# Second expert product of a mixture layer with the weights as the stationary side

## The chip, the cores and the metric

The program runs on one core of a Trainium2 chip. Its time is the device time of one execution, in microseconds (us). Of the kernel before, three timed runs gave 2428.65, 2429.38 and 2433.24 us; the median is 2429.38.

## What is computed

The program is a whole network on 3136 tokens (16 images of 14 x 14) of 256 channels: convolutions, a convolutional attention, and two layers of attention with a feed-forward part each. Only the last part, a mixture of experts, is touched:

```
logits = x @ router_w ; probs = softmax(logits)
gate = max(probs) ; idx = argmax(probs)
# each expert takes the first C = 3136/8 = 392 tokens that chose it, in "slots"
h = relu(expert_inputs @ w1[e] + b1[e])        # [392, 256] @ [256, 1024]
expert_outputs = h @ w2[e] + b2[e]             # [392, 1024] @ [1024, 256]
out[token] = gate[token] * expert_outputs[its slot]   # 0 for a token with no slot
x = x + out
```

There are 8 experts. All of it is float32. The experts' input is the layer-normalised x; their output is added to x itself.

## The kernel before

The function is `moe_ffn`. It is written out by hand as one program for each engine; semaphores alone set the order between engines, and each engine works through its own list strictly in order. In memory x lies with channels on partitions: 2 chunks of 128 channels (KC = 2), 3136 tokens along a row.

*Start.* The sync engine loads the router, b1 and b2 (L1992 to L1994, semaphore consts_in), then the weights of experts 0 and 1 (L1997, L1998). TensorE waits for all three small loads at the head of its list (consts_in at 48), takes the column means of the router (L2060) and turns b1 into columns (L2062). The vector engine subtracts the means from the router (L2182), and with that TensorE turns the tokens into rows and scores them (L2073, L2076), 128 tokens at a time. Slot numbers are worked out on the vector engine, and GpSimd scatters the normalised rows by slot into the DRAM tensor expert_in with 25 indirect DMAs (L2046). A row holds 256 channels, the token's number and its gate.

*Experts.* 392 slots are 4 groups (s) of 98 slots. Expert e uses buffers e % 2 of the weights w1 and w2, of the incoming rows ein, of the hidden layer h and of the result y. In order of TensorE's list:

- first product (L2104): for each of 8 blocks f of 128 hidden units, 2 matmuls into one of the banks 0 to 3, stationary a 128x128 piece of w1, moving the 392 slots. The activation engine adds b1 and clips (L2163) into h.
- second product (L2115): for each slot group s, 8 matmuls, stationary the 98 slots of h, moving the 256 channels of w2, into bank 6 or 7. The result has slots on partitions.
- between slot groups 2 and 3, `turn_in` (L2089): 8 transposes that bring the next expert's rows ein to channels on partitions (banks 4 and 5), copied out by the activation engine (L2152).

The vector engine makes the token numbers and gates of the expert (L2269 to L2275), multiplies b2 by the gates (b2g, L2278), and then, for each slot group, y = product x gate + b2g (L2284, semaphore y_ready). GpSimd scatters each slot group of y into out_rows by token number (L2053). When y_ready is full the sync engine loads ein and the weights of expert e + 2. Experts 0, 1 and 6, 7 are written out in TensorE's list, the others are in a loop.

*End.* When all scatters have landed (L2017), out_rows is loaded back in 8 pieces (L2019), turned by TensorE (L2128), added to x by the vector engine (L2292) and stored.

A float32 matmul shows in the trace as two records, each with a weight load of its own, a transpose as one.

Of the kernel before, what the change touches and what calls it, by code (L numbers as in the profile page):

```python
# [14 lines left out]
P = 128  # L15
# [14 lines left out]
def steps(eng, n, body):  # L30

    body(0)
    if n > 1:
        with eng.Fori(1, n) as i:
            body(i)
# [1877 lines left out]
def moe_ffn(nc, x, expert_in, out_rows, y_dram, mean_w, w, ident):  # L1913
# [15 lines left out]
    with Scope(nc, "moe") as S:  # L1929
# [14 lines left out]
        sent_f, sent = S.sb("sent_f", [P, NTILES]), S.sb("sent", [P, NTILES], U32)  # L1944
        w1 = [S.sb(f"w1_{p}", [P, KC, F]) for p in range(2)]
        w2 = [S.sb(f"w2_{p}", [P, KF, C]) for p in range(2)]
        b1_rows, b1, b2 = S.sb("b1_rows", [E * KF, P]), S.sb("b1", [P, E * KF]), S.sb("b2", [ST, E, C])
        ein = [S.sb(f"ein{p}", [ST, 4, CW]) for p in range(2)]
        token, gates = [S.sb(f"token{p}", [ST, 4], U32) for p in range(2)], [S.sb(f"gates{p}", [ST, 4]) for p in range(2)]
        vacant, token_f = S.sb("vacant", [ST, E, 4]), S.sb("token_f", [ST, 4])  # L1950
        b2g = S.sb("b2g", [ST, 4, C])
        ein_t = [S.sb(f"ein_t{p}", [P, KC, CAP]) for p in range(2)]
        h = [S.sb(f"h{p}", [P, KF, CAP]) for p in range(2)]
        y = [S.sb(f"y{p}", [ST, 4, C]) for p in range(2)]
# [15 lines left out]
        onehot_ready, counted, slots_ready = S.sem("onehot_ready"), S.sem("counted"), S.sem("slots_ready")  # L1970
        ein_turned, ein_ready, h_done, h_ready = S.sem("ein_turned"), S.sem("ein_ready"), S.sem("h_done"), S.sem("h_ready")
        token_step = S.sem("token_step")
        meta_ready, b2g_ready, y_done, y_ready = S.sem("meta_ready"), S.sem("b2g_ready"), S.sem("y_done"), S.sem("y_ready")
        back_turned, x_done = S.sem("back_turned"), S.sem("x_done")
        block = S.block()

# [13 lines left out]
        @block.sync  # L1990
        def _(sp):
            sp.dma_start(router[:, :, :], w["router_w"].rearrange("(k p) e -> p k e", p=P)).then_inc(consts_in, 16)  # L1992
            sp.dma_start(b1_rows[:, :], w["b1"].rearrange("e (f p) -> (e f) p", p=P)).then_inc(consts_in, 16)  # L1993
            sp.dma_start(b2[:, :, :], w["b2"].unsqueeze(0).broadcast_to([ST, E, C])).then_inc(consts_in, 16)  # L1994

            def weights(e, p):
                sp.dma_start(w1[p][:, :, :], w["w1"][bass.ds(e, 1)].rearrange("o (k p) f -> p (o k) f", p=P)).then_inc(w_in[p], 16)  # L1997
                sp.dma_start(w2[p][:, :, :], w["w2"][bass.ds(e, 1)].rearrange("o (k p) d -> p (o k) d", p=P)).then_inc(w_in[p], 16)  # L1998
            for p in range(2):
                weights(p, p)  # L2000
            sp.wait_ge(scattered, 16 * NTILES)
            for p in range(2):
                sp.dma_start(ein[p][:, :, :], slots_of(p)).then_inc(ein_in[p], 16)

            def body(i):
                for p in range(2):
                    e = 2 * i + p
                    sp.wait_ge(y_ready, 4 * (e + 1))
                    sp.wait_ge(ein_turned, e + 1)
                    sp.wait_ge(meta_ready, e + 1)  # L2010
                    sp.dma_start(ein[p][:, :, :], slots_of(e + 2)).then_inc(ein_in[p], 16)
                    weights(e + 2, p)
            body(0)
# [43 lines left out]
        def _(pe):  # L2057
# [1 line left out]
            for k in range(KC):  # L2059
                mm = nc.tensor.matmul(count_ps[:, 0:E], mean_w[:, :], router[:, k, :], start=(k == 0), stop=(k == KC - 1))  # L2060
            mm.then_inc(mean_done, 1)
            nc.tensor.transpose(bank[5][:, 0:E * KF], b1_rows[:, :], ident[0:E * KF, 0:E * KF]).then_inc(b1_turned, 1)  # L2062

            for g in range(NG):
                if g == 0:
# [27 lines left out]
            pe.wait_ge(ein_in[0], 16)  # L2093
            turn_in(0)

            def experts(i, last):
                for p in range(2):
                    e = 2 * i + p
                    pe.wait_ge(w_in[p], 32 * (i + 1))
                    pe.wait_ge(ein_ready, e + 1)  # L2100
                    for f in range(KF):
                        wait(pe, h_ready, KF * e + f - 3)
                        for k in range(KC):
                            mm = nc.tensor.matmul(a_ps[f % 4][:, 0:CAP], w1[p][:, k, f * P:(f + 1) * P], ein_t[p][:, k, :],  # L2104
                                                  start=(k == 0), stop=(k == KC - 1))
                        mm.then_inc(h_done, 1)
                    for s in range(4):
                        if s == 3 and not (last and p == 1):
                            pe.wait_ge(ein_in[1 - p], 16 * (i + 1 + p))
                            turn_in(1 - p)  # L2110
                        wait(pe, y_ready, 4 * e + s - 1)
                        for f in range(KF):
                            if s == 0:
                                pe.wait_ge(h_ready, KF * e + f + 1)
                            mm = nc.tensor.matmul(y_ps[s % 2][0:ST, 0:C], h[p][:, f, s * ST:(s + 1) * ST], w2[p][:, f, :],  # L2115
                                                  start=(f == 0), stop=(f == KF - 1))
                        mm.then_inc(y_done, 1)
            experts(0, False)
            with pe.Fori(1, E // 2 - 1) as i:
                experts(i, False)  # L2120
            experts(E // 2 - 1, True)

            for i in range(NPIECE):
                pe.wait_ge(back_in[i], 16)
# [7 lines left out]
        def _(act):  # L2132
            act.preload_act_table_set(LN_EXP)
            act.wait_ge(b1_turned, 1)
            nc.scalar.activation(b1[:, :], bank[5][:, 0:E * KF], ACT.Copy).then_inc(b1_ready, 1)
            for g in range(NG):
                js = group(g)
                a, b = js[0], js[-1] + 1
# [18 lines left out]
            def experts(i, last):  # L2157
                for p in range(2):
                    e = 2 * i + p
                    wait(act, y_done, 4 * (e - 1))  # L2160
                    for f in range(KF):
                        act.wait_ge(h_done, KF * e + f + 1)
                        nc.scalar.activation(h[p][:, f, :], a_ps[f % 4][:, 0:CAP], ACT.Relu, bias=b1[:, bass.ds(e * KF + f, 1)]).then_inc(h_ready, 1)  # L2163
# [9 lines left out]
        def _(dve):  # L2173
# [85 lines left out]
            chain.wait()  # L2259
            nc.vector.reciprocal(rows[:, :, C + 1], total[:, :]).then_inc(gate_ready, 1)  # L2260

            dve.wait_ge(consts_in, 48)

            def experts(i):
                for p in range(2):
# [8 lines left out]
                    nc.vector.tensor_copy(token[p][:, :], token_f[:, :])  # L2274
                    nc.vector.tensor_copy(gates[p][:, :], ein[p][:, :, C + 1]).then_inc(meta_ready, 1)  # L2275
                    dve.wait_ge(meta_ready, e + 1)
                    for s in range(4):
                        ins = nc.vector.tensor_scalar(b2g[:, s, :], b2[:, bass.ds(e, 1), :].rearrange("p o c -> p (o c)"),  # L2278
                                                      gates[p][:, s:s + 1], None, ALU.mult)
                    ins.then_inc(b2g_ready, 1)  # L2280
                    dve.wait_ge(b2g_ready, e + 1)
                    for s in range(4):
                        dve.wait_ge(y_done, 4 * e + s + 1)
                        nc.vector.scalar_tensor_tensor(y[p][:, s, :], y_ps[s % 2][0:ST, 0:C], gates[p][:, s:s + 1], b2g[:, s, :],  # L2284
                                                       ALU.mult, ALU.add).then_inc(y_ready, 1)
            steps(dve, E // 2, experts)

            for i in range(NPIECE):
                dve.wait_ge(back_turned, i + 1)
# [50 lines left out]
```

## Time and profile before

| | |
|---|---|
| median of three timed runs | 2429.38 us |
| profiled execution | 2433.36 us |
| its span, first to last instruction | 2431.3 us |
| mean granted clock of TensorE | 0.874 |
| TensorE busy over the span | 1915.6 us, 79% |
| vector engine busy | 1685.6 us, 69% |
| mixture stage, first DMA issue | 2105.93 us |
| first expert's first product | 2196.05 us |
| second product of the last expert ends | 2397.97 us |

The mixture stage is the last 325 us of the span, and the eight experts are 202 us of it. Times inside the trace count from the start of the span. Nothing outside `moe_ffn` is edited, so the shares over the whole span say little here; the views that are cut to the last 325 us do.

### The profile page before, as it was taken

How to read it: one execution, taken by the hardware profiler on the slowest of the kernel's cores; microseconds unless marked ns; L12 is line 12 of the kernel's file. 1: busy time of each engine (PE TensorE's matmuls, PEld its weight loads, DVE VectorE, ACT ScalarE, POOL GpSimd, SP SyncE). 2: the span in 40 equal slices, each digit the busy share in tenths (PEclk: the TensorE clock that was granted, in tenths of full speed). 3: DMA queues.
4: the chain of work that ended last, by engine and by line, in shares of the span. 5: the costliest groups of instructions: out<-in, count | busy, mean ns of one | idle time of the engine just before them, and what ended most of it. 6: DMA issues, size and time to landing. Idle time of an engine off the chain costs nothing. (4 is left out here: it accounts for less than half of the span.)

```text
span 2431.3 us, 48421 instructions
## 1 busy us (share of the span) xinstructions
PE 1915.6 (79%) x17730; PEld 1571.1 (65%) x17730; DVE 1685.6 (69%) x7003; ACT 669.6 (28%) x1492; POOL 463.1 (19%) x667
## 2 busy tenths in 40 slices
PE   7595899984569788797787977878869699728996
PEld 3364688872468677676676766767758577526674
DVE  3333666634999999989989998999995577321112
ACT  2342355543222131121311213112120255321210
POOL 2002344330020202202112021120220300041110
PEclk8786999996789899898998989989879899858997
DMA  2222444413500000000000000000000333312434
GB/s 59 80 84 58 113 109 101 103 23 99 113 6 5 2 6 1 6 6 1 6 2 6 5 2 6 1 6 2 1 2 1 74 84 83 96 52 69 139 99 116
DMA packets 90505, 111.10 MB, mean 46 GB/s; under 512 B 27166, under 2 KB 79070, under 8 KB 89534
## 3 DMA queue, kind: packets, MB, share of 16 engines
q1 hardware_dynamic: 84752, 99.88, 15.6%
q0 software_dynamic: 3344, 6.53, 0.8%
q8 instruction: 144, 2.36, 0.4%
q10 hardware_dynamic: 2176, 1.61, 0.2%
q14 instruction: 89, 0.73, 0.1%
HBM read 70.63 MB, written 33.83 MB: 43 GB/s over the span
## 5 line engine op out<-in xcount | busy, mean ns | idle before, releaser
L1618 PE MATMUL peer_out_ps<-peer_g,peer_up 128*128 128x256 f32 (+1 forms) x1664 | 378.1, 392 | 84.6 <-issue 76.7
L1618 PEld LDWEIGHTS peer_out_ps<-peer_g,peer_up 128*128 128x128 f32 x1664 | 326.0, 203 | 133.0 <-issue 84.7
L1583 PE MATMUL peer_x_ps<-peer_xc,peer_dt 128*128 128x256 f32 (+1 forms) x1664 | 355.2, 374 | 26.8 <-DMA peer_up<-in_L_ffn_expert_up_dram 19.0
L1583 PEld LDWEIGHTS peer_x_ps<-peer_xc,peer_dt 128*128 128x128 f32 x1664 | 308.2, 192 | 68.6 <-issue 28.6
L1547 POOL TENSOR_TENSOR peer_g<-peer_g,peer_qt 128x512 f32<-128x512 f32 x96 | 153.9, 1644 | 802.8 <-ACT peer_qt L1709 802.8
L1687 ACT ACTIVATE peer_g<-peer_x_ps 128x512 f32<-128x512 f32 (+1 forms) x208 | 119.1, 572 | 645.7 <-PE peer_x_ps L1583 645.6
L1284 DVE TENSOR_REDUCE l_attn_mx<-l_attn_s_ps 98x4 f32<-98x392 f32 (+1 forms) x320 | 175.0, 560 | 140.3 <-PE l_attn_s_ps L1054 101.0
L1607 PE MATMUL peer_x_ps<-peer_oh_h,peer_oh_a 128*128 128x32 bf16 x3136 | 171.5, 181 | 112.3 <-DVE peer_oh_l L1875 96.4
L1607 PEld LDWEIGHTS peer_x_ps<-peer_oh_h,peer_oh_a 128*128 128x128 bf16 x3136 | 165.1, 99 | 129.5 <-DVE peer_oh_l L1875 64.7
L1868 DVE TENSOR_TENSOR peer_oh_a<-peer_a_t,peer_iota_f 128x8192 bf16<-128x8192 bf16 x49 | 216.7, 4423 | 1.3
L1205 ACT ACTIVATE l_attn_pt<-l_attn_st_ps 98x392 f32<-98x392 f32 x320 | 148.1, 491 | 146.4 <-PE l_attn_st_ps L1067 145.6
L1732 DVE FIND_INDEX8 peer_i<-peer_v,peer_sc 128x8 uint32<-128x64 f32 (+1 forms) x800 | 175.4, 236 | 0.0
L1608 PE MATMUL peer_x_ps<-peer_oh_l,peer_oh_a 128*128 128x32 bf16 x3136 | 170.6, 181 | 0.0
L1608 PEld LDWEIGHTS peer_x_ps<-peer_oh_l,peer_oh_a 128*128 128x128 bf16 x3136 | 165.2, 99 | 0.9
L1050 PE MATMUL l_attn_s_ps<-l_attn_stk,l_attn_stq 96*98 96x196 bf16 (+1 forms) x768 | 112.4, 243 | 31.5 <-DMA l_attn_stk<-l_attn_pieces_k_dram 19.0
L2284 DVE SCALAR_TENSOR_TENSOR moe_y<-moe_b_ps,moe_gates,moe_b2g 98x256 f32<-98x256 f32 x32 | 15.5, 484 | 174.3 <-PE moe_b_ps L2115 174.3
L979 POOL TENSOR_SCALAR_AFFINE_SELECT l_attn_pt<-l_attn_pt 98x196 f32<-98x196 f32 (+1 forms) x192 | 98.6, 519 | 136.6 <-ACT l_attn_pt L1205 135.3
L1067 PE MATMUL l_attn_st_ps<-l_attn_stq,l_attn_stk 98*98 98x196 bf16 (+1 forms) x768 | 111.5, 243 | 9.2 <-ACT l_attn_pt L1205 4.5
L1727 DVE MAX8 peer_v<-peer_sc 128x8 f32<-128x64 f32 (+1 forms) x800 | 106.0, 215 | 11.1 <-issue 9.8
L2115 PE MATMUL moe_b_ps<-moe_w,moe_h 128*98 128x256 f32 x512 | 113.0, 379 | 0.0
L2115 PEld LDWEIGHTS moe_b_ps<-moe_w,moe_h 128*98 128x98 f32 x512 | 83.9, 165 | 26.9 <-issue 1.3
L1050 PEld LDWEIGHTS l_attn_s_ps<-l_attn_stk,l_attn_stq 96*98 96x98 bf16 x768 | 71.7, 128 | 43.7 <-DVE l_attn_mx L1284 22.0
(318 smaller groups left out, 3520.8 us busy)
## 6 DMA issues: line engine op xcount, KB each, us to landing
moe_w<-in_L_ffn_w_dram SPq DMA_DIRECT2D x16, 1024.0 KB, 8.7
l_attn_pieces_q_dram<-l_attn_pieces_q SPq DMA_DIRECT2D x16, 294.0 KB, 4.6
l_attn_pieces_k_dram<-l_attn_pieces_k SPq DMA_DIRECT2D x16, 294.0 KB, 3.2
l_attn_stq<-l_attn_pieces_q_dram SPq DMA_DIRECT2D x16, 294.0 KB
l_attn_stk<-l_attn_pieces_k_dram SPq DMA_DIRECT2D x16, 294.0 KB
peer_g<-n_L_ffn_expert_down_dram SPq DMA_DIRECT2D x8, 512.0 KB
peer_up<-in_L_ffn_expert_up_dram SPq DMA_DIRECT2D x2, 2048.0 KB
moe_expert_in<-l_blank SPq DMA_DIRECT2D x16, 197.5 KB
```

The costliest lines, as they stand in the source:

```text
L1050: mm = nc.tensor.matmul(out[:, j, :], stq[n % NB][0:KS, spot(h), t * TH:(t + 1) * TH], stk[n % NB][0:KS, spot(h), 0:nb * TH], start=(j == ...
L1205: nc.scalar.activation(pt[g % NPT][:, f * FW:(f + 1) * FW], st_ps[i % 2][0:TH, 0:FW], ACT.Exp).then_inc(exp_done, 1)
L1284: nc.vector.tensor_reduce(mx[n % 2][:, hs[0]:hs[0] + len(hs), t], s_ps[i % 2][0:TH, 0:FW].rearrange("p (h j) -> p h j", j=nb * TH), AX_X, ...
L1547: nc.gpsimd.tensor_tensor(g[:, :, ts], g[:, :, ts], m_copy[q % 2].rearrange("p (t j) -> p j t", j=J), ALU.mult).then_inc(g_done_late, 1)
L1583: mm = nc.tensor.matmul(x_ps[b][:, jj * CT:jj * CT + cols], dt[:, k, 2 * jp + jj, :], xc[p][:, k, 0:cols], start=(k == 0), stop=(k == KC - 1))
L1607: nc.tensor.matmul(x_ps[q][:, i * J:(i + 1) * J], oh_a[hb % 2][:, t, :], oh_h[hb % 2][:, t, :], start=True, stop=False)
L1608: mm = nc.tensor.matmul(x_ps[q][:, i * J:(i + 1) * J], oh_a[hb % 2][:, t, :], oh_l[hb % 2][:, t, :], start=False, stop=True)
L1618: mm = nc.tensor.matmul(out_ps[:, m * CT:m * CT + cols], up[:, j, m * P:(m + 1) * P], g[:, j, 0:cols], start=(j == 0), stop=(j == J - 1))
L1687: nc.scalar.activation(g[:, 2 * jp:2 * jp + 2, 0:cols], x_ps[jp % 4][:, 0:2 * CT].rearrange("p (j t) -> p j t", j=2)[:, :, 0:cols], ACT.Ge ...
L1732: last = nc.vector.max_index(indices[:, q, r], values[:, q, r], source)
L1868: nc.vector.tensor_tensor(view(oh_a[q]), spread(a_t, P), number(P), ALU.is_equal)
L2115: mm = nc.tensor.matmul(y_ps[s % 2][0:ST, 0:C], h[p][:, f, s * ST:(s + 1) * ST], w2[p][:, f, :], start=(f == 0), stop=(f == KF - 1))
```

## The change

The second product swaps its sides: the stationary piece is 128x128 of w2 (128 hidden units, 128 channels), and all 392 slots of h move. There are two such products per expert, one for each chunk k of 128 channels, into banks 6 and 7. The result has channels on partitions, so b2 becomes a column of 128 and is added by the vector engine as it moves the bank into a new buffer yt; b2 is loaded as 16 rows of 128 and turned like b1. The scatter needs slots on partitions, so yt is turned back: `turn_out`, 8 transposes into banks 4 and 5, and the vector engine multiplies by the gate on the way into y (`slots_out`). For expert e, turn_out stands in expert e + 1, after block f = 1 of its first product, and slots_out after the token work of e + 1; for the last expert both stand at the end. turn_in moves between the two channel chunks and waits for y_ready of the expert before, since it uses the same banks. The sync engine asks for the next rows and weights at y_done instead of y_ready.

```diff
-            sp.dma_start(b2[:, :, :], w["b2"].unsqueeze(0).broadcast_to([ST, E, C])).then_inc(consts_in, 16)
+            sp.dma_start(b2_rows[:, :], w["b2"].rearrange("e (k p) -> (e k) p", p=P)).then_inc(consts_in, 16)
...
-                    sp.wait_ge(y_ready, 4 * (e + 1))
+                    sp.wait_ge(y_done, KC * (e + 1))
...
+            def turn_out():
+                for half in range(2):
+                    for s in range(2 * half, 2 * half + 2):
+                        for k in range(KC):
+                            o = (s % 2) * C + k * P
+                            mm = nc.tensor.transpose(t_ps[half][0:ST, o:o + P], yt[:, k, s * ST:(s + 1) * ST], ident[:, :])
+                    mm.then_inc(y_turned, 1)
...
                         mm.then_inc(h_done, 1)
-                    for s in range(4):
-                        if s == 3 and not (last and p == 1):
+                        if f == 1 and not first:
+                            pe.wait_ge(yt_ready, KC * e)
+                            turn_out()
+                    for k in range(KC):
+                        if k == 1 and not (last and p == 1):
                             pe.wait_ge(ein_in[1 - p], 16 * (i + 1 + p))
+                            wait(pe, y_ready, 4 * e)
                             turn_in(1 - p)
-                        wait(pe, y_ready, 4 * e + s - 1)
+                        wait(pe, yt_ready, KC * e)
                         for f in range(KF):
-                            if s == 0:
+                            if k == 0:
                                 pe.wait_ge(h_ready, KF * e + f + 1)
-                            mm = nc.tensor.matmul(y_ps[s % 2][0:ST, 0:C], h[p][:, f, s * ST:(s + 1) * ST], w2[p][:, f, :],
+                            mm = nc.tensor.matmul(y_ps[k][:, 0:CAP], w2[p][:, f, k * P:(k + 1) * P], h[p][:, f, :],
                                                   start=(f == 0), stop=(f == KF - 1))
                         mm.then_inc(y_done, 1)
...
+            pe.wait_ge(yt_ready, KC * E)
+            pe.wait_ge(y_ready, 4 * (E - 1))
+            turn_out()
...
+            def slots_out(e, p):
+                for s in range(4):
+                    dve.wait_ge(y_turned, 2 * e + s // 2 + 1)
+                    nc.vector.tensor_scalar(y[p][:, s, :], t_ps[s // 2][0:ST, (s % 2) * C:(s % 2 + 1) * C], gates[p][:, s:s + 1], None,
+                                            ALU.mult).then_inc(y_ready, 1)
...
-                    for s in range(4):
-                        ins = nc.vector.tensor_scalar(b2g[:, s, :], b2[:, bass.ds(e, 1), :].rearrange("p o c -> p (o c)"),
-                                                      gates[p][:, s:s + 1], None, ALU.mult)
...
-                        nc.vector.scalar_tensor_tensor(y[p][:, s, :], y_ps[s % 2][0:ST, 0:C], gates[p][:, s:s + 1], b2g[:, s, :],
-                                                       ALU.mult, ALU.add).then_inc(y_ready, 1)
+                    if not (isinstance(e, int) and e == 0):
+                        slots_out(e - 1, 1 - p)
+                    for k in range(KC):
+                        dve.wait_ge(y_done, KC * e + k + 1)
+                        wait(dve, y_turned, 2 * e)
+                        nc.vector.tensor_scalar(yt[:, k, :], y_ps[k][:, 0:CAP], b2[:, bass.ds(e * KC + k, 1)], None, ALU.add).then_inc(yt_ready, 1)
             steps(dve, E // 2, experts)
+            slots_out(E - 1, 1)
```

TensorE's list before, from the end of the first product of expert 0 to the third block of expert 1's. A name b4 is bank 4; the form at the end is that of the output.

```order
L2104 MATMUL moe_b3_ps<-moe_ein_t0,moe_w1_0 128x392 x2
L2115 MATMUL moe_b6_ps<-moe_w2_0,moe_h0 98x256 x8
L2115 MATMUL moe_b7_ps<-moe_w2_0,moe_h0 98x256 x8
L2115 MATMUL moe_b6_ps<-moe_w2_0,moe_h0 98x256 x8
L2089 MATMUL moe_b4_ps<-net_ident,moe_ein1 128x98 x4
L2089 MATMUL moe_b5_ps<-net_ident,moe_ein1 128x98 x4
L2115 MATMUL moe_b7_ps<-moe_w2_0,moe_h0 98x256 x8
L2104 MATMUL moe_b0_ps<-moe_ein_t1,moe_w1_1 128x392 x2
L2104 MATMUL moe_b1_ps<-moe_ein_t1,moe_w1_1 128x392 x2
L2104 MATMUL moe_b2_ps<-moe_ein_t1,moe_w1_1 128x392 x2
```

The same place now:

```order
L2116 MATMUL moe_b3_ps<-moe_ein_t0,moe_w1_0 128x392 x2
L2131 MATMUL moe_b6_ps<-moe_h0,moe_w2_0 128x392 x8
L2092 MATMUL moe_b4_ps<-net_ident,moe_ein1 128x98 x4
L2092 MATMUL moe_b5_ps<-net_ident,moe_ein1 128x98 x4
L2131 MATMUL moe_b7_ps<-moe_h0,moe_w2_0 128x392 x8
L2116 MATMUL moe_b0_ps<-moe_ein_t1,moe_w1_1 128x392 x2
L2116 MATMUL moe_b1_ps<-moe_ein_t1,moe_w1_1 128x392 x2
L2104 MATMUL moe_b4_ps<-net_ident,moe_yt 98x128 x4
L2104 MATMUL moe_b5_ps<-net_ident,moe_yt 98x128 x4
L2116 MATMUL moe_b2_ps<-moe_ein_t1,moe_w1_1 128x392 x2
```

32 matmuls of 256 columns became 16 of 392, and the transposes out of yt (L2104 of the new text) stand behind two blocks of the next first product.

The vector engine's list before, for expert 1:

```order
L2269 SCALAR_TENSOR_TENSOR moe_token_f<-moe_ein1,moe_vacant 98x4
L2272 TENSOR_TENSOR moe_token_f<-moe_token_f,moe_ein1 98x4
L2274 CAST moe_token1<-moe_token_f 98x4
L2275 COPY moe_gates1<-moe_ein1 98x4
L2278 TENSOR_SCALAR moe_b2g<-moe_b2,moe_gates1 98x256 x4
L2284 SCALAR_TENSOR_TENSOR moe_y1<-moe_b6_ps,moe_gates1,moe_b2g 98x256
L2284 SCALAR_TENSOR_TENSOR moe_y1<-moe_b7_ps,moe_gates1,moe_b2g 98x256
L2284 SCALAR_TENSOR_TENSOR moe_y1<-moe_b6_ps,moe_gates1,moe_b2g 98x256
L2284 SCALAR_TENSOR_TENSOR moe_y1<-moe_b7_ps,moe_gates1,moe_b2g 98x256
```

And now:

```order
L2295 SCALAR_TENSOR_TENSOR moe_token_f<-moe_ein1,moe_vacant 98x4
L2298 TENSOR_TENSOR moe_token_f<-moe_token_f,moe_ein1 98x4
L2300 CAST moe_token1<-moe_token_f 98x4
L2301 COPY moe_gates1<-moe_ein1 98x4
L2287 TENSOR_SCALAR moe_y0<-moe_b4_ps,moe_gates0 98x256 x2
L2287 TENSOR_SCALAR moe_y0<-moe_b5_ps,moe_gates0 98x256 x2
L2308 TENSOR_SCALAR moe_yt<-moe_b6_ps,moe_b2 128x392
L2308 TENSOR_SCALAR moe_yt<-moe_b7_ps,moe_b2 128x392
```

The slots of expert 0 (y0) are written in expert 1's turn, before the two channel halves of expert 1 itself.

## Rows read from the trace of the kernel before

**Rows 1.** Chain of waits: start us, length us, what, from the first expert on
```profile
2196.05 12.93 PE moe_b_ps L2104 x32
2208.98 10.36 PE moe_b_ps L2115 x48
2219.34 0.68 PE moe_b_ps L2089 x8
2220.02 3.46 PE moe_b_ps L2115 x16
2223.47 10.53 PE moe_b_ps L2104 x32
...
2384.16 10.37 PE moe_b_ps L2115 x48
```

**Rows 2.** Stretches: length; busy us PE, PEld, DVE, ACT, POOL; PE clock; DMA; GB/s
```profile
2106.00:2112.00 6.00, 0.02 (x1) 0.02 (x1) 0.06 (x1) 1.22 (x1) 1.37 (x7) 0.50 0.62 192
2112.00:2145.00 33.00, 30.80 (x155) 30.49 (x155) 12.88 (x61) 12.32 (x33) 0.00 (x0) 0.50 0.34 119
2196.00:2198.00 2.00, 1.95 (x3) 1.18 (x4) 0.00 (x0) 0.00 (x0) 0.00 (x0) 0.50 0.00 0
2222.00:2247.00 25.00, 25.00 (x105) 17.29 (x104) 3.68 (x12) 5.58 (x10) 3.79 (x4) 1.00 0.37 116
```

**Rows 3.** Instructions on the PSUM banks: ns min/median/max, first and last start
```profile
L2115 PEld LDWEIGHTS moe_b_ps<-moe_w,moe_h x512: 163/165/167, 2208.5 to 2397.4; 128*98 128x98 f32 x171
L2104 PEld LDWEIGHTS moe_b_ps<-moe_ein_t,moe_w x256: 190/190/338, 2196.0 to 2383.3; 128*128 128x128 f32 x128
L2089 PE MATMUL moe_b_ps<-net_ident,moe_ein x64: 245/248/396, 2193.4 to 2369.9; 98*128 98x98 f32 x64
```

**Rows 4.** Timeline at the end of the last first product: start, length, instruction
```profile
2384.19 0.59 ACT L2163 ACTIVATE moe_h<-moe_b_ps,moe_b 128x392 f32<-128x392 f32 x1 [0.73 <-PE moe_b_ps L2104]
```

**Rows 5.** Timeline at the start of the stage
```profile
2106.97 0.57 SPq L1994 DMA_DIRECT2D moe_b<-in_L_ffn_b_dram  x1
2111.98 1.02 PE L2060 MATMUL moe_b_ps<-moe_router,net_mean_w 128*128 128x8 f32 x4 [7.89 <-DMA moe_b<-in_L_ffn_b_dram]
2113.47 0.69 PE L2073 MATMUL moe_b_ps<-net_ident,net_x 128*128 128x128 f32 x2 [0.17 <-DVE moe_centred L2182]
```

**Rows 6.** DMA issues (KB each, us to landing), and the group of GpSimd's scatters
```profile
l_wn<-in_L_conv_Wf_dram SPq DMA_DIRECT2D x1, 64.0 KB, 2.0
moe_w<-in_L_ffn_w_dram SPq DMA_DIRECT2D x16, 1024.0 KB, 8.7
L2046 POOL DMA_INDIRECT moe_expert_in<-moe_rows,moe_sent x25 | 24.4, 977 | 56.0 <-DVE moe_rows L2260 48.7 <-issue 7.3
```

**Rows 7.** Timeline of the last expert's second product and after, and the chain's wait
```profile
2383.99 13.98 PE L2115 MATMUL moe_b_ps<-moe_w,moe_h 128*98 128x256 f32 x64
2387.65 0.48 DVE L2284 SCALAR_TENSOR_TENSOR moe_y<-moe_b_ps,moe_gates,moe_b2g 98x256 f32<-98x256 f32 x1 [11.65 <-PE moe_b_ps L2115]
2388.96 0.95 POOL L2053 DMA_INDIRECT moe_out_rows<-moe_y,moe_token  x1 [13.57 <-DVE moe_y L2284]
2398.01 0.48 DVE L2284 SCALAR_TENSOR_TENSOR moe_y<-moe_b_ps,moe_gates,moe_b2g 98x256 f32<-98x256 f32 x1 [2.97 <-PE moe_b_ps L2115]
2398.79 0.94 POOL L2053 DMA_INDIRECT moe_out_rows<-moe_y,moe_token  x1 [2.50 <-DVE moe_y L2284]
2401.57 0.02 SPq L2017
```

**Rows 8.** Groups of the vector engine: busy, mean ns of one | idle before
```profile
L1250 DVE TENSOR_TENSOR l_attn_xn<-l_attn_xn,l_attn_rstd 128x392 f32<-128x392 f32 x32 | 17.9, 558 | 9.9 <-ACT l_attn_rstd L1165 9.9
L2284 DVE SCALAR_TENSOR_TENSOR moe_y<-moe_b_ps,moe_gates,moe_b2g 98x256 f32<-98x256 f32 x32 | 15.5, 484 | 174.3 <-PE moe_b_ps L2115 174.3
L506 DVE TENSOR_SCALAR l_lin<-l_c_ps,l_scale,l_shift 64x392 f32<-64x392 f32 x8 | 5.5, 693 | 0.0
L507 DVE TENSOR_SCALAR l_ypad<-l_lin 64x392 f32<-64x392 f32 x8 | 2.9, 361 | 0.3
```

More of the change, by code:

```diff
@@ L1946, in moe_ffn @@
         w2 = [S.sb(f"w2_{p}", [P, KF, C]) for p in range(2)]
-        b1_rows, b1, b2 = S.sb("b1_rows", [E * KF, P]), S.sb("b1", [P, E * KF]), S.sb("b2", [ST, E, C])
+        b1_rows, b1 = S.sb("b1_rows", [E * KF, P]), S.sb("b1", [P, E * KF])
+        b2_rows, b2 = S.sb("b2_rows", [E * KC, P]), S.sb("b2", [P, E * KC])
         ein = [S.sb(f"ein{p}", [ST, 4, CW]) for p in range(2)]
@@ L1950, in moe_ffn @@
         vacant, token_f = S.sb("vacant", [ST, E, 4]), S.sb("token_f", [ST, 4])
-        b2g = S.sb("b2g", [ST, 4, C])
+        yt = S.sb("yt", [P, KC, CAP])
         ein_t = [S.sb(f"ein_t{p}", [P, KC, CAP]) for p in range(2)]
@@ L1972, in moe_ffn @@
         token_step = S.sem("token_step")
-        meta_ready, b2g_ready, y_done, y_ready = S.sem("meta_ready"), S.sem("b2g_ready"), S.sem("y_done"), S.sem("y_ready")
+        meta_ready, y_done, y_ready = S.sem("meta_ready"), S.sem("y_done"), S.sem("y_ready")
+        yt_ready, y_turned = S.sem("yt_ready"), S.sem("y_turned")
         back_turned, x_done = S.sem("back_turned"), S.sem("x_done")
@@ L2061, in _ @@
             mm.then_inc(mean_done, 1)
-            nc.tensor.transpose(bank[5][:, 0:E * KF], b1_rows[:, :], ident[0:E * KF, 0:E * KF]).then_inc(b1_turned, 1)
+            nc.tensor.transpose(bank[5][:, 0:E * KF], b1_rows[:, :], ident[0:E * KF, 0:E * KF])
+            nc.tensor.transpose(bank[5][:, E * KF:E * KF + E * KC], b2_rows[:, :], ident[0:E * KC, 0:E * KC]).then_inc(b1_turned, 1)
             for g in range(NG):
@@ L2098, in experts @@
                     e = 2 * i + p
+                    first = isinstance(e, int) and e == 0
                     pe.wait_ge(w_in[p], 32 * (i + 1))
@@ L2134, in _ @@
             act.wait_ge(b1_turned, 1)
-            nc.scalar.activation(b1[:, :], bank[5][:, 0:E * KF], ACT.Copy).then_inc(b1_ready, 1)
+            nc.scalar.activation(b1[:, :], bank[5][:, 0:E * KF], ACT.Copy)
+            nc.scalar.activation(b2[:, :], bank[5][:, E * KF:E * KF + E * KC], ACT.Copy).then_inc(b1_ready, 1)
             for g in range(NG):
@@ L2159, in experts @@
                     e = 2 * i + p
-                    wait(act, y_done, 4 * (e - 1))
+                    wait(act, y_done, KC * (e - 1))
                     for f in range(KF):
@@ L2260, in _ @@
             nc.vector.reciprocal(rows[:, :, C + 1], total[:, :]).then_inc(gate_ready, 1)
-            dve.wait_ge(consts_in, 48)
+            dve.wait_ge(b1_ready, 1)
+            def slots_out(e, p):
[3 more added lines that the diff above has]
+                                            ALU.mult).then_inc(y_ready, 1)
             def experts(i):
@@ L2276, in experts @@
                     dve.wait_ge(meta_ready, e + 1)
-                    for s in range(4):
-                        ins = nc.vector.tensor_scalar(b2g[:, s, :], b2[:, bass.ds(e, 1), :].rearrange("p o c -> p (o c)"),
-                                                      gates[p][:, s:s + 1], None, ALU.mult)
[L2280 to L2283, printed above, removed]
-                        nc.vector.scalar_tensor_tensor(y[p][:, s, :], y_ps[s % 2][0:ST, 0:C], gates[p][:, s:s + 1], b2g[:, s, :],
-                                                       ALU.mult, ALU.add).then_inc(y_ready, 1)
+                    if not (isinstance(e, int) and e == 0):
[4 more added lines that the diff above has]
+                        nc.vector.tensor_scalar(yt[:, k, :], y_ps[k][:, 0:CAP], b2[:, bass.ds(e * KC + k, 1)], None, ALU.add).then_inc(yt_ready, 1)
             steps(dve, E // 2, experts)
+            slots_out(E - 1, 1)
             for i in range(NPIECE):
```

## The prediction

> **What bounds the kernel now.** I read four views, from the coarse to the fine. The chain of waits, in order of time, comes first: from 2196 to 2398 us, through all eight experts, every link of it is TensorE, and the links join end to start. One expert is 10.53 us for the first product (32 records, two to each float32 matmul), 10.36 + 3.46 us for the second (64 records) and 0.68 us for the eight transposes of the next expert's rows, 25.03 us in all [rows 1]. So whatever TensorE does not have to do there comes off the time, and nothing else on another engine does, unless TensorE is made to wait for it. The stretches with the granted clock say the same: in 25 us TensorE is busy 25.00 us at clock 1.00, the vector engine 3.68, the activation engine 5.58, GpSimd 3.79 [rows 2]. The view of the instructions on the PSUM banks gives the price of a record and of its weight load [rows 3]. The timelines of the two ends of the stage show what stands before the first expert and after the last [rows 5, 7].
>
> **Second product.** Before: 64 records of 256 columns in 13.82 us, 216 ns each, 0.84 ns a column. After: 16 matmuls, 32 records, of 392 columns, in the same form as the first product (128x128 stationary, 392 columns moving), and 32 of those take 10.53 us, 329 ns each and again 0.84 ns a column [rows 1]. The gain is one of columns, 16,384 against 12,544: with 98 slots as the stationary side 30 of the 128 columns of the array stood empty, with 128 channels none does. The weight load grows from 165 to 190 ns but stays under a record of 329 ns, as it does in the first product [rows 3]. 8 x (13.82 - 10.53) = 26.3 us less. Bounds: the form is in the trace, so I allow 0.1 us an expert at the joints, 25.5 to 26.5. The waits for h_ready move from every 0.43 us to every 0.66 us, and the activation that they wait for takes 0.59 us in both; the last one is asked for 14 records after the first product ends, 4.6 us, and it is there after 0.62 [rows 4]. No cost.
>
> **Turning back, seven times inside the next expert.** Eight transposes of 128 columns. The eight of turn_in, 98 columns each, add 0.68 us between two products, 85 ns each though one lasts 248 [rows 1, 3]; by columns 128/98 x 85 = 111 ns, 0.89 us for eight. From below it is 0.68 (pace set by the issue, not the columns), from above eight full durations in a row, 8 x 0.25 = 2.0. I take 0.9, since turn_in is the same operation in the same surroundings: 7 x 0.9 = 6.3 us more, ends 4.8 and 14.
>
> The rows show such transposes overlapping, so they are priced by pace. The Trainium skill (TensorE: Matmul & The Clock Gate, Part 4: PE-mode transpose) gives about 275 ns for one inside a kernel; laid end to end that would be 2.2 us an expert, an estimate from that page, and 9 us more than in my sum. This trace disagrees for turn_in, with 85 ns of pace against 248 of duration.
>
> **Does TensorE wait for it?** turn_out stands behind four records of the next first product, 4 x 0.33 = 1.32 us after the second product ended. By then the vector engine must have moved the second channel half out of PSUM. It starts 0.04 us after the last matmul today [rows 7] and its work is new in this form: one operand from PSUM, 128x392, float32. Nearest rows: 361 ns for such a shape out of SBUF, 558 for two operands of 128x392, 693 for a two-step operation out of PSUM [rows 8]. I take 0.56; with 0.69 it is still 0.6 us early. It stands ahead of the token work in the vector engine's program, so nothing is queued before it. The next wait, turn_in for y_ready, comes after the whole first product and half of the second, some 15 us after turn_out, while slots_out is four operations of at most 0.5 us [rows 8]. The scatters of an expert now run in the first third of the next one, at one per 1.27 us [rows 6]; their buffers are asked for again one expert later. The weights are asked for at y_done, half a microsecond earlier than at y_ready, and land after 8.7 us [rows 6], while the period shrinks only from 25.0 to 22.6. So the covers hold, all of them by at least 0.6 us. The removed b2g work, four short operations an expert under the first product, was hidden and gives nothing back.
>
> **Start of the stage.** TensorE waits until 2111.98 for b2, 784 KB broadcast to 98 partitions, issued at 2106.97 [rows 5]. Now b2 is 16 rows of 512 bytes, 8 KB. Transfers of 64 KB land 2.0 us after their issue in this kernel [rows 6], so consts_in should be full at about 2109.3, 2.7 us earlier. From below nothing is gained (the router load, 8 KB in small pieces, could be the late one), from above 3.0 (the load of b1 issued half a microsecond before must land too). One more transpose of 16 rows stands before router_ready, where TensorE had 0.17 us to spare [rows 5], so 0.1 us back. Everything behind it, scores, slots, 25 scatters at 1.27 us, is a chain of waits that moves as a whole. The clock there is already at 0.50 before the stage starts and stays [rows 2], so nothing changes in it. I take 2.6 us less.
>
> **Tail, once.** Before: the last matmul ends at 2397.97, the vector engine takes 0.48, GpSimd starts its last scatter at 2398.79 and the wait for the scatters ends at 2401.57, 3.60 us after the matmul [rows 7]. The other three scatters were done during the second product, one slot group every 3.45 us. Now all four come after it: 0.04 + 0.56 for the second channel half into SBUF; 0.03 + 0.75 until the first four transposes are through (weight load 0.17, duration 0.25, three at 0.11); 0.50 for the first slots into y; 0.84 until GpSimd starts, as it does at the first scatter of an expert today (2388.13 to 2388.96 [rows 7]); then three more scatters at 1.27 = 3.81 [rows 6]; and 2.77 from the start of the last to its landing. Together 9.30 us, so 5.7 more. Ends: 5.0 with 0.30 in place of 0.84 and the smallest vector times, 6.3 with the largest. The eighth turn_out is in here. From the load of out_rows on nothing changes.
>
> **Sum** against the profiled execution (2433.36 us, span 2431.3): -26.3 + 6.3 - 2.6 + 5.7 = -16.9 us, 2416.5. That execution stands 4.0 us above the median of the three timed runs, 2429.38, which spread over 4.6 us while the stage changed here has the same instructions in each; I subtract from the median: 2412.5 us.
>
> **Rivals.**
> A. The transposes of turn_out don't overlap: 2.0 us an expert instead of 0.9, 7.8 us more, 2420.3. For it: their stationary side comes from a tile just written and their bank pair was last read by the activation engine. Against it: turn_in is under the same conditions. 0.06.
> B. The load of b2 was not what held the start, and the router's small pieces were: 2.6 us are not gained, 2415. For it: a name in the trace covers only the transfer that ended last, and nothing shows when the router landed. Against it: 784 KB from the end of their issue at 2107.54 to 2111.98 are 181 GB/s, close to the 192 GB/s that the stretch from 2106 to 2112 shows [rows 2, 5]. 0.12.
> C. TensorE waits at turn_out because the channel half comes late. It takes more than 1.32 us from the last matmul to yt_ready; each 0.5 us over it costs 3.5, so 2416 to 2420. Only an operation of twice the 0.69 us gets there. 0.04.
> D, the other side: the clock falls. After turn_out (and turn_in) TensorE's clock drops from 2.4 to 1.2 GHz. A fall has a price in this trace: the first expert's first product, begun at clock 0.50, takes 12.93 us instead of 10.53, 2.40 more [rows 1, 2]. One fall at each of the seven turn_out gives back 16.8, which is no change (2429.3); with eight transposes more at turn_in falling too, that is fifteen falls, 36 us, and 2448. It is slower from the eighth fall on. Against it: the stretch of 25 us with turn_in in its middle stays at 1.00 [rows 2], and turn_out adds only 0.9 us of the same kind, with matmuls on both sides. 0.04, half of it past the eighth fall.
>
> Rival D is what a rule would make of it: the Trainium skill (TensorE: Matmul & The Clock Gate, Part 4: PE-mode transpose) says that the full clock does not engage for transposes, since they do not count as busy in the same way. By that rule the trace agrees where only transposes and 8-column products run (0.50 throughout), and does not where they stand among long matmuls.
>
> **How the numbers follow.** My forecast, 2412.5, has 0.72; A 0.06, B 0.12, C 0.04, D 0.04, and 0.02 is left for something in the tail or elsewhere that I don't see. The forecast's own range, from the ends of its terms that can fall together (start 1 to 3 us, turn_out 4.8 to 8, tail 5.0 to 6.3), and 1 us for the spread of a median of three, is 2409 to 2416. To hold 8 in 10 it reaches to B and to the near part of C: 2408.5 to 2417.5. What counts as a change is 0.2%, 4.9 us, about what a measurement of this kernel can tell from none. Faster than 2424.5: the forecast, B, C, A, together 0.94; within: the half of D up to the eighth fall and half of the rest, 0.03; slower: the other halves, 0.03.
>
> **What would show it.** In the changed kernel's chain: the second product as 8 x 32 records in 10.5 us, an expert in 22.6 us, turn_out with 0.9 us between two parts of the first product and no idle time of TensorE before it. At the start: L2062 (the first matmul of the stage) some 2.7 us earlier after the barrier. At the end: four scatters spaced 1.27 us after the last matmul and 9.3 us until the loads of out_rows. Wrong if an expert takes over 23.5 us, if the clock in it is under 1.00, if the matmul at the start comes at the same distance from the barrier, or if the tail is outside 8.5 to 10 us.

## The result and the profile after

The changed kernel takes 2413.3 us (median of 6 runs), the one before 2429.02 in the same series: ratio 0.993, 95% interval 0.9911 to 0.9949. Two later series gave 0.9902 (0.9863 to 0.9941) and 0.9919 (0.9889 to 0.9949). It is faster by 0.7 to 1.0% by the three ratios and by 16 to 20 us by the medians; 2412.5 had been forecast. One execution, of the kernel both_ends below, took 4707.02 us where all others lie between 2401 and 2439; it is left out of every median and ratio here, and its cause is open.

Single runs of either kernel differ by up to 19 us, so the terms are read inside the stage. Its four pieces, in us, each the difference of two starts in a timeline:

| profile | first issue to first matmul | to first product of expert 0 | to load of out_rows | to end of span | stage |
|---|---|---|---|---|---|
| before | 6.05 | 84.07 | 205.57 | 29.7 | 325.4 |
| after | 2.84 | 83.83 | 190.95 | 29.4 | 307.0 |

The chain of waits after, from expert 0 on (start us, length us, what); L2131 is the second product, L2092 turn_in, L2104 turn_out:

```profile
2186.20 12.78 PE moe_b_ps L2116 x32
2198.98 5.27 PE moe_b_ps L2131 x16
2204.25 0.68 PE moe_b_ps L2092 x8
2204.92 5.29 PE moe_b_ps L2131 x16
2210.22 2.63 PE moe_b_ps L2116 x8
2212.85 0.88 PE moe_b_ps L2104 x8
2213.72 7.90 PE moe_b_ps L2116 x24
...
2357.50 10.55 PE moe_b_ps L2131 x32
```

Against [rows 1]: the second product is 5.27 + 5.29 = 10.56 us where it was 13.82, turn_out is 0.88 between two parts of the first product, every link is TensorE and none waits. An expert is 22.64 us instead of 25.03. The clock stays up. Over one period of an expert the vector engine is busy 3.38 us in 10 operations, where it was 3.68 us in 12 (the last line of [rows 2], whose 25.00 us are one period of the kernel before; columns as there):

```profile
2210.22:2232.86 22.64, 22.64 (x81) 13.62 (x81) 3.38 (x10) 5.58 (x10) 3.80 (x4) 1.00 0.38 128
```

How much cover turn_out has is in the timeline. The second product ends at 2210.22 by the chain, and the vector engine's move of the second channel half ends at 2210.88:

```profile
2210.25 0.63 DVE L2308 TENSOR_SCALAR moe_yt<-moe_b_ps,moe_b 128x392 f32<-128x392 f32 x1 [5.26 <-PE moe_b_ps L2131]
2212.69 1.04 PE L2104 MATMUL moe_b_ps<-net_ident,moe_yt 128*98 128x128 f32 x8
```

Two blocks of the first product are eight records, 2.63 us, and the move is through 0.66 us after the second product: 1.97 us are to spare in the chain.

The start, in the timeline, for [rows 5]:

```profile
2099.53 0.40 SPq L1994 DMA_DIRECT2D moe_router<-in_L_ffn_router_w_dram  x1
2100.57 0.58 SPq L1996 DMA_DIRECT2D moe_b_rows<-in_L_ffn_b_dram  x1
2102.37 1.02 PE L2062 MATMUL moe_b_ps<-moe_router,net_mean_w 128*128 128x8 f32 x4 [4.68 <-DMA moe_b_rows<-in_L_ffn_b_dram]
2103.86 0.69 PE L2076 MATMUL moe_b_ps<-net_ident,net_x 128*128 128x128 f32 x2
```

TensorE still waits for a bias load (the name stands for b1_rows and for b2_rows), but b2 is now 8 KB (L1996), and the first matmul comes 1.80 us after its issue. The additional transpose costs nothing: 1.49 us from L2062 to L2076, as before. The tail, for [rows 7]:

```profile
2357.33 10.70 PE L2131 MATMUL moe_b_ps<-moe_h,moe_w 128*128 128x392 f32 x32
2368.18 0.62 DVE L2308 TENSOR_SCALAR moe_yt<-moe_b_ps,moe_b 128x392 f32<-128x392 f32 x1 [4.64 <-PE moe_b_ps L2131]
2368.86 1.08 PE L2104 MATMUL moe_b_ps<-net_ident,moe_yt 128*98 128x128 f32 x8 [0.83 <-DVE moe_yt L2308]
2369.54 1.66 DVE L2287 TENSOR_SCALAR moe_y<-moe_b_ps,moe_gates 98x256 f32<-98x256 f32 x4 [0.74 <-PE moe_b_ps L2104]
2370.85 0.95 POOL L2055 DMA_INDIRECT moe_out_rows<-moe_y,moe_token  x1 [15.56 <-DVE moe_y L2287]
2372.10 0.94 POOL L2055 DMA_INDIRECT moe_out_rows<-moe_y,moe_token  x1 [0.31 <-issue]
2373.35 0.95 POOL L2055 DMA_INDIRECT moe_out_rows<-moe_y,moe_token  x1 [0.30 <-issue]
2374.60 0.95 POOL L2055 DMA_INDIRECT moe_out_rows<-moe_y,moe_token  x1 [0.30 <-issue]
2377.15 6.50 SPq L2021 DMA_DIRECT2D moe_back<-moe_out_rows  x8
```

The last matmul ends at 2368.03. The vector engine is through with all four slot groups at 2371.20, but GpSimd's fourth scatter starts only at 2374.60: the tail is a queue on GpSimd. 9.12 us to the load of out_rows, where it was 3.65.

### The profile page after: what moved, and what is told of

It is laid out like the page before. It is cut to its first block and busy times, and to the rows that moved or that the text cites. A ratio compares the mean times of both kernels' runs of the same rounds, so it can differ in the third digit from the quotient of the medians.

```text
span 2406.5 us, 48028 instructions
## 1 busy us (share of the span) xinstructions
PE 1891.0 (79%) x17539; PEld 1540.1 (64%) x17539; DVE 1684.0 (70%) x6987; ACT 670.1 (28%) x1493; POOL 462.3 (19%) x667
## 5 line engine op out<-in xcount | busy, mean ns | idle before, releaser
L1732 DVE FIND_INDEX8 peer_i<-peer_v,peer_sc 128x8 uint32<-128x64 f32 (+1 forms) x800 | 166.0, 219 | 0.0
L2308 DVE TENSOR_SCALAR moe_yt<-moe_b_ps,moe_b 128x392 f32<-128x392 f32 x16 | 10.0, 625 | 146.1 <-PE moe_b_ps L2131 146.1
L1088 PE MATMUL l_attn_o_ps<-l_attn_pt,l_attn_va 98*32 98x196 f32 (+1 forms) x1536 | 91.9, 309 | 9.5 <-DVE l_attn_o L1291 8.9
L1067 PEld LDWEIGHTS l_attn_st_ps<-l_attn_stq,l_attn_stk 98*98 98x98 bf16 x768 | 70.7, 125 | 39.6 <-ACT l_attn_pt L1205 13.4
```

Source lines behind the costliest of these rows:

```text
L1067: mm = nc.tensor.matmul(out[:, j, :], stk[n % NB][:, spot(h), u * TH:(u + 1) * TH], stq[n % NB][:, spot(h), t0 * TH:HW], start=(j == 0), s ...
L1732: last = nc.vector.max_index(indices[:, q, r], values[:, q, r], source)
```

## The experiments

All were compared by the four pieces of the stage:

| profile | first matmul | to first product | to load of out_rows | to end | stage |
|---|---|---|---|---|---|
| after_again | 2.95 | 84.13 | 190.94 | 30.8 | 308.8 |
| after_long | 3.00 | 84.14 | 191.05 | 28.9 | 307.1 |
| start_alone | 2.45 | 83.84 | 205.71 | 29.5 | 321.5 |
| turn_first | 2.99 | 84.53 | 197.90 | 28.2 | 313.6 |
| turn_four | 2.90 | 84.12 | 209.47 | 28.9 | 325.4 |
| halves_all | 2.78 | 84.35 | 191.48 | 28.2 | 306.8 |
| narrow | 2.90 | 84.57 | 190.93 | 27.5 | 305.9 |
| tail_halves | 2.91 | 84.96 | 187.88 | 29.3 | 305.1 |
| both_ends | 2.00 | 84.40 | 188.55 | 27.9 | 302.8 |
| both_again | 1.70 | 84.58 | 188.46 | 28.2 | 302.9 |

The third piece is the steady one: the unedited changed kernel shows it three times within 0.11 us. What moves in it is the first product of expert 0, which begins at clock 0.50 (in the changed kernel 0.50 up to 2190, 0.88 from there to 2191 and 1.00 behind it) and takes 12.52 to 13.24 us over all these profiles with the same instructions. Without it the piece is 178.17, 178.18 and 178.18 us in the three profiles of the changed kernel; where a difference is given "less expert 0's first product" below, it is taken so. The last piece, the stores of the output, varies by 3 us over all these profiles.

**The changed kernel again** (after_again and after_long, no edit).

> The changed kernel once more, unedited. Two theories on why its timed runs spread over 11 us (2408.4 to 2419.5) where those of the kernel before spread over 5. Theory 1: the spread comes from the part of the program that was not edited (the first layers, up to the first load of the attention part at 225.9 us in the one profile of the changed kernel and 233.9 us in that of before), and the mixture stage, from its first DMA issue to the end of the span, is 307.0 us again, to within 0.5 us, whatever the whole time is. Theory 2: the new overlap in the stage is unsteady (scatters and weight loads at the same time), and the stage differs by several us between the profiles.

Four runs, 2403.9 to 2419.3, median 2409.98. The stage began at 2104.28, 4.8 us later than in the first profile, and 13 runs of the kernel before spread over 19 us in this series: the spread belongs to the unedited part and to both kernels (theory 1), though the stage itself moved by 1.8 us, more than the 0.5 expected, 1.4 of it in the stores. The piece with the new overlap stood still (190.94 against 190.95), so theory 2 falls.

> The changed kernel unedited, timed in five rounds on one chip beside the next kernel and the kernel before, because single runs of all of them differ by up to 19 us in the part that was not edited. Theory: the difference to the kernel before is the difference of the stages in the profiles, 325.4 less 307.0 to 308.8, so 16.6 to 18.4 us, ratio 0.9925 to 0.993; stage again 307 to 309. Rival: something outside the stage gained or lost too; then the ratio of many runs lies away from 0.993 by more than its interval.

Six runs, median 2410.0, ratio 0.9919 (0.9889 to 0.9949). The stages differ by 16.6 to 18.4 us in three profiles, a ratio of 0.9932 to 0.9924, inside the interval. No sign of a gain or loss outside the stage; the interval would hide one of up to some 7 us.

**The start alone** (start_alone, edit of the kernel before):

```diff
-            sp.dma_start(b2[:, :, :], ...).then_inc(consts_in, 16)      # before the weights
+            sp.dma_start(b2[:, :, :], ...).then_inc(b2_in, 16)          # behind the weights
-            pe.wait_ge(consts_in, 48)
+            pe.wait_ge(consts_in, 32)
```

> The kernel before, with one part of the change alone: the broadcast load of b2 no longer stands in front of TensorE (it is issued behind the weights, with a semaphore of its own, and the vector engine waits for it before the experts). The experts are as before. My theory: the start term was a wait for these 784 KB alone, so the stage gets 3.2 us shorter (from the first issue to the first matmul 2.8 us instead of 6.05), stage 322.2 instead of 325.4 us, whole time 2426. Rival: the router's small pieces or the crowd of weight loads behind them hold the start; then the first matmul comes at 4 to 6 us after the first issue and the stage is 324 to 325 us.

The first matmul comes 2.45 us after the first issue, the experts are as before (205.71), the stage is 3.9 us shorter (3.2 expected); ten timed runs against 13 give 0.9981 (0.9962 to 0.9999), median 2426.83. 3.6 of the 6.05 us were the wait for the broadcast b2; the router's pieces and the weight loads issued behind it held nothing up beyond that. The rival falls. With b2_rows still in front the changed kernel starts 0.4 to 0.55 us later than this one profile (2.84 to 3.00 in three), so the 8 KB of b2 do not look free either.

**turn_out without cover** (turn_first, edit of the changed kernel): the call moved from behind block f = 1 to before block f = 0.

> The changed kernel with the eight transposes back (turn_out) ahead of the next expert's first product instead of behind its second block: the cover of 1.32 us is gone. My theory: TensorE then waits, seven times, for the move of the second channel half out of PSUM, 0.04 + 0.62 us after the last matmul, plus the start of a weight load and the drain, 0.8 to 0.9 us each time as at the end of the stage (0.83 us of idle there): 5.6 to 6.3 us more, an expert 23.5 us instead of 22.65, stage 312.6 to 313.3 instead of 307.0. Rival: the move is no matter at this place, since the sequencer hides it: stage within 1 us of 307.0.

```profile
2219.93 0.62 DVE L2308 TENSOR_SCALAR moe_yt<-moe_b_ps,moe_b 128x392 f32<-128x392 f32 x1 [5.26 <-PE moe_b_ps L2131]
2220.70 1.05 PE L2104 MATMUL moe_b_ps<-net_ident,moe_yt 128*98 128x128 f32 x8 [0.81 <-DVE moe_yt L2308]
```

6.95 us more, and 7.2 in the piece less expert 0's first product (185.38 against 178.17), 1.03 for each of seven: TensorE is idle for 0.7 to 0.9 us, and the eight transposes take 1.05 to 1.08 us in the chain where they took 0.88. Above the 5.6 to 6.3 expected, since I had counted the idle time alone. The cover that was taken away is 2.63 us, two blocks of four records each, and not 1.32 as I had written; one block, 1.31 us, would by these rows still cover the 0.66 us that the move needs, but no run shows that. The cover is worth 7 of the 16 to 20 us.

**turn_out four times over** (turn_four, edit: the eight transposes listed four times before each signal, in the seven calls inside the experts).

> The changed kernel with each of the seven turn_out inside the experts done four times over (32 transposes in a row, the same result written four times; the last turn_out, at the end, once). Theory of pace: a transpose of 128 columns costs 0.11 us of TensorE wherever it stands, so 7 x 24 x 0.109 = 18.3 us more, stage 325.3 us, clock 1.00 throughout the experts. Rival, the clock: 3.5 us of nothing but transposes let TensorE's clock fall to 1.2 GHz; then at least 2.4 us more for each expert, 35 us or more in all, and a granted clock under 1.00 in the stretches of the experts. Rival, durations: if they did not overlap it would be 0.27 each, 46 us.

The chain of one expert and a stretch:

```profile
2236.92 2.63 PE moe_b_ps L2116 x8
2239.56 3.49 PE moe_b_ps L2104 x32
2243.05 7.90 PE moe_b_ps L2116 x24
```
```profile
2235.00:2260.00 25.00, 25.00 (x104) 16.06 (x103) 3.47 (x10) 5.58 (x10) 3.78 (x4) 1.00 0.35 117
```

32 transposes in 3.49 us, 109 ns each, clock 1.00: 18.5 us more in the third piece, 18.3 less expert 0's first product; 18.3 expected. Rivals A (no overlap) and D (the clock falls) both fall, and D by four times the dose.

**Twice the records and weight loads** (halves_all, edit: each matmul of the second product as two of 196 columns).

> The changed kernel with every second-product matmul cut in two, 196 columns each with a weight load of its own: the same columns, twice the records and weight loads (64 records an expert, as many as in the kernel before). Theory of columns: 64 x 196 x 0.84 ns + 3 ns each = 10.7 us instead of 10.55, so 1 to 2 us more over eight experts, 192 to 193 us from the first product to the load of out_rows instead of 190.9. Rival, weight loads: a record can't be shorter than the 190 ns of its weight load; then 12.2 us an expert, 13 us more, 204. That rival would also make the number of weight loads, halved by the change, a cause of the gain.

```profile
2227.10 5.31 PE moe_b_ps L2133 x32
```
```profile
L2133 PEld LDWEIGHTS moe_b_ps<-moe_h,moe_w x512: 190/190/192, 2203.9 to 2373.6; 128*128 128x128 f32 x171
```

64 records of 196 columns take 5.31 + 5.33 = 10.64 us, 166 ns each, though each weight load lasts 190: loads overlap each other. The rival's 12.2 us falls. It is 0.5 us more in all (0.6 less expert 0's first product), under the 1 to 2 expected: 2.5 ns for each of the 256 additional records. The halved number of records and weight loads is therefore 0.6 us of the gain at most.

**A narrower stationary side** (narrow, edit: 14 of 16 matmuls of a second product load 98 of the 128 channels; 30 channels are left out of the sum there).

> The changed kernel with 14 of the 16 matmuls of each second product loading only 98 of the 128 channels as their stationary piece (30 channels are left out of the sum there). Theory: the time goes by the columns that move, 392, and not by how full the array is, so the second product takes 10.5 us again and the stage is unchanged within 0.3 us from first product to the load of out_rows (190.9): 98 stationary columns in the kernel before cost as much per moving column as 128, and the emptiness was the loss. Rival: a narrower stationary side is cheaper in itself, 98/128 of the time, 8.1 us an expert; then the stage is 16 to 19 us shorter.

```profile
L2132 PEld LDWEIGHTS moe_b_ps<-moe_h,moe_w x256: 165/165/192, 2202.6 to 2371.3; 128*98 128x98 f32 x112, 128*128 128x128 f32 x16
```
```profile
2225.71 5.27 PE moe_b_ps L2132 x16
```

The weight load is back at 165 ns, the product takes 5.27 us for 16 records as with 128 channels, the third piece is 190.93, and the rival's 8.1 us falls. In this product the time goes by the columns that move. Together with the last run this settles the main term.

**Both ends.** tail_halves changes the last expert (shortened):

```diff
+    for part in range(2):                       # 196 slots each; banks 6, 7 and then 0, 1
+        for k in range(KC):
+            if part == 1 and k == 1:
+                pe.wait_ge(yt_ready, KC * e + 2)
+                pe.wait_ge(y_ready, 4 * e)
+                turn_out((0,))                  # slot groups 0 and 1
+            for f in range(KF): matmul(..., w2[...], h[p][:, f, cols])
...
+            pe.wait_ge(yt_ready, KC * E + 2)
+            turn_out((1,))
```

> The changed kernel, the last expert's second product in two halves of 196 slots (second half in banks 0 and 1), the first half turned back after the first product of the second half, so that two of the four last scatters are done under it. Theory: the tail is a queue on GpSimd, four scatters at 1.25 us. Two of them go under the product; TensorE ends 0.6 us later (four transposes moved in, records of 196 columns), and from its last matmul to the load of out_rows there are 5.9 us instead of 9.1. From the first product of expert 0 to that load 188.3 us instead of 190.9. Rival: GpSimd is late anyway through the vector engine, which serves both halves in order; then it is 190 to 191.

```profile
2371.39 0.95 POOL L2055 DMA_INDIRECT moe_out_rows<-moe_y,moe_token  x1 [11.95 <-DVE moe_y L2302]
2372.64 0.94 POOL L2055 DMA_INDIRECT moe_out_rows<-moe_y,moe_token  x1 [0.31 <-issue]
2374.67 0.95 POOL L2055 DMA_INDIRECT moe_out_rows<-moe_y,moe_token  x1 [1.08 <-DVE moe_y L2302]
2375.93 0.95 POOL L2055 DMA_INDIRECT moe_out_rows<-moe_y,moe_token  x1 [0.30 <-issue]
2378.47 6.87 SPq L2021 DMA_DIRECT2D moe_back<-moe_out_rows  x8
```

187.88 us, 3.1 less; 2.8 of it is the edit's (175.35 against 178.17 less expert 0's first product), 2.6 were expected. TensorE's last matmul ends at 2372.70, and 5.77 us later out_rows is loaded (5.9 expected, 9.12 in the changed kernel). both_ends adds to it a start in which TensorE waits for the router alone and turns the biases after the first group of tokens (shortened):

```diff
-            sp.dma_start(b1_rows[:, :], ...).then_inc(consts_in, 16)
+            sp.dma_start(b1_rows[:, :], ...).then_inc(bias_in, 16)      # b2_rows too
-            pe.wait_ge(consts_in, 48)
+            pe.wait_ge(consts_in, 16)
```

> The changed kernel with both ends worked on. At the start the biases b1 and b2 no longer stand before the first matmul: TensorE waits for the router alone, and turns the biases after the first four groups of tokens. At the end the last expert's second product is done in two halves of 196 slots, the second half in banks 0 and 1, and the first half is turned back, gated and scattered while the second is computed. Expected as the sum of the two single kernels: 0.9 us at the start and 2.6 at the end, stage 303.5 to 305.3 instead of 307.0 to 308.8, so 3.5 us under the changed kernel and some 20 to 22 us under the one before (2408 against 2429.5). Rival: the two halves cost TensorE more than the scatters give back, and the whole is within 1 us of the changed kernel.

> The kernel with both ends worked on, unedited, in the same rounds. Theory: its stage is 302.8 us again to within 1.5 us, 4 to 5 us under the changed kernel, and so is the median, 2407 to 2409 where the changed kernel has 2411 to 2413. The difference is as large as what the timed runs can tell, so the stage decides. Rival: same median as the changed kernel, the gain of the two ends being lost in the stores of the output, whose landing varied by 3 us between profiles.

The stage is 302.8 and 302.9 us, 4 to 6 under the changed kernel and under the 303.5 to 305.3 expected. The first matmul comes after 2.00 and 1.70 us. The experts are as in tail_halves (175.33 and 175.34 less expert 0's first product, which took 13.22 and 13.12 here). Timed: medians 2408.82 (five runs) and 2406.56 (six), ratios to the kernel before 0.9909 (0.9879 to 0.994) and 0.9904 (0.9878 to 0.9929). In the second series, side by side, the changed kernel had 2410.0, so 3.4 us; the intervals overlap, and that this kernel is the fastest is shown by the stage, not by the timed runs.

## Why the prediction was right

By its own steps, with the first profile:

| term | forecast | measured |
|---|---|---|
| second product, 8 experts | -26.3 | 8 x (10.56 - 13.82) = -26.1 |
| turn_out, 7 inside | +6.3 | 7 x 0.88 = +6.2 |
| waits of TensorE in the experts | 0 | 0 |
| start | -2.6 | -3.2 |
| tail | +5.7 | 9.12 - 3.65 = +5.5 |
| rest of the stage | 0 | -0.2 before the experts, -0.3 after them, -0.2 in them (expert 0's first product, 12.78 for 12.93) |
| stage | -16.9 | -18.4; -16.6 and -18.3 in two more profiles |

- *The main term* was a form already in the trace, used at its own price, and came out within 1%. The reason behind it (columns that move) is shown by halves_all and narrow, to 0.6 us.
- *turn_out* by pace instead of duration: 109 ns against a duration of 273 in the trace, the very pair that turn_in had offered with 85 and 248. The Trainium skill's 275 ns (TensorE: Matmul & The Clock Gate, Part 4: PE-mode transpose) agrees with the duration; as a price it would have put 9 us too much.
- *The cover* was miscounted. turn_out stands behind two blocks, and a block is 2 matmuls of two records: eight records, 2.63 us, and not "four records", 1.32 us, so the 1.32 us in rival C was wrong too. The move out of PSUM takes 0.62 us, not 0.56, inside my bounds of 0.36 to 0.69. So 1.97 us are to spare where I had 0.6. That TensorE does not wait came out right with the wrong length of cover, because the slip was on the safe side; turn_first shows what the absence of cover costs.
- *The start* was sized 0.6 too small. I added the small load's 2.0 us (a load of 64 KB) to the issue of b2 at 1.04 us after the router's and then 0.3 of caution, and gave back 0.1 for the transpose; the trace has 1.80 us from the issue of b2_rows and nothing for the transpose. What remains of the start, a bias load in front of the first matmul, is taken away in both_ends.
- *The tail* was right in sum and by parts: GpSimd 0.83 after the first y, a scatter each 1.25 us (1.27 forecast), 2.5 to landing (2.77 forecast).
- *The rivals.* A and D are excluded by turn_four, B by start_alone, C by the chain. On D the Trainium skill (TensorE: Matmul & The Clock Gate, Part 4: PE-mode transpose) has the rule that the full clock does not engage for transposes; it does not hold for 32 of them in 3.49 us among long matmuls, where the clock was 1.00 and stayed there. Whether transposes alone would raise the clock no run shows. For the transposes and 8-column products at the start of the stage, which begin at clock 0.50 and stay there [rows 2], no run here speaks against it.
- *The range.* The ends of the terms, all added to the median, give 2409.7 to 2417.2 before the 1 us for the spread; the 2416 of the forecast's own range lies below that upper end, and why those ends could not fall together is not said. The three medians, 2413.3, 2409.98 and 2410.0, lie inside either.

What the sum did not hold is in the timed runs: the part before the stage differs by up to 10 us between profiles (first issue at 2098.5 to 2108.6 us with the same instructions), so the agreement of 2413.3 with 2412.5 to 1 us is closer than such a series can tell: it is luck in part, and the two later series have medians 2.5 us below the forecast.

## What to carry to other kernels

Count the columns that move through TensorE, with the larger free dimension as the moving side and a full 128 as the stationary one, and count what must be turned back; price both by pace, from rows of the same form. A reordering that moves work behind the next unit pays once at the end, where all that used to be spread lies in one queue; count the cover in records from the chain of the changed kernel; look for the slowest engine of that queue, and cut the last unit in two. When the edited stage is an eighth of a program whose rest varies by more than the gain, compare the stage.

## What the runs showed of the hardware

- Float32 weight loads of 128 columns overlap each other: 190 ns long, one every 166 ns (halves_all: 32 records in 5.31 us).
- The vector engine adding a per-partition value to 128x392 out of PSUM takes 625 ns, longer than two operands of that size, 558 ns, out of SBUF alone [rows 8] or with one of them in PSUM (L2316):

```profile
L2308 DVE TENSOR_SCALAR moe_yt<-moe_b_ps,moe_b 128x392 f32<-128x392 f32 x16 | 10.0, 625 | 146.1 <-PE moe_b_ps L2131 146.1
L2287 DVE TENSOR_SCALAR moe_y<-moe_b_ps,moe_gates 98x256 f32<-98x256 f32 x32 | 13.3, 476 | 13.6 <-PE moe_b_ps L2104 13.6
L2316 DVE TENSOR_TENSOR net_x<-net_x,moe_b_ps 128x392 f32<-128x392 f32 x16 | 8.3, 558 | 15.0 <-PE moe_b_ps L2147 15.0
```

  In tail_halves the same addition on 196 columns takes 419 ns. The pair gives 1.05 ns a column and 213 fixed, and by that 482 for 256 columns, where the multiplication on 98 partitions took 476. What makes it longer than the two operands is not shown. The Trainium skill (VectorE: DVE Perf Modes, The TRN2 errata, its cycle table for PSUM to SBUF) makes it 120 + 392 cycles at 0.96 GHz, 533 ns as an estimate; the trace is 17% above.
- GpSimd starts the first scatter of an expert 0.83 us after its data (about 2370.02 to 2370.85 at the end of the changed kernel), and each of the following 1.25 us after the one before when their data are there. A later scatter that has to wait starts sooner after its data: 0.30 us in the kernel before (2398.49 to 2398.79 [rows 7]) and 0.31 in tail_halves. Why the first one takes longer is not shown.
